# Two pieces of TensorE's work moved inside one step of an attention stage

## The reference

```
x = x + xattn0(ctx, layernorm(x))     # 16 heads of 16: softmax(q k^T / 4) v, then w_out and b_out
x = x + ffn0(layernorm(x))            # gate logits = xn @ gate_w.T + gate_b; the top 2 of 8 are counted,
                                      # and relu(xn @ W_e + b_e) is averaged over experts by those counts
x = x + xattn1(layernorm(x), ctx)     # one head of 256, with the mask
x = x + ffn1(layernorm(x))            # 8 experts, top 2, softmax weights
```

## Time and profile before

| | us |
|---|---|
| median of 3 runs | 973.59 (972.66 to 981.06) |
| the profiled execution | 976.29 |
| its span, first to last instruction | 974.4 |
| first stage, steps with all work (300 to 350 us of the span): PE busy | 50.00 of 50.00 |
| the same: DVE, ACT, POOL busy | 43.22, 37.10, 28.86 of 50.00 |

### The profile page before, as it was taken

The page is one execution under the profiler, slowest core; times in us unless marked ns, Lnnn a source line. Parts: engine busy times, 40 slices in busy tenths (PEclk is TensorE's granted clock), DMA queues, the critical chain, the costliest instruction groups (busy, mean ns, idle before and its releaser), DMA issues. The chain is left out here.

```text
span 974.4 us, 31409 instructions
## 1 busy us (share of the span) xinstructions
PE 896.9 (92%) x10664; PEld 666.5 (68%) x10664; DVE 728.6 (75%) x2063; ACT 550.2 (56%) x1112; POOL 540.1 (55%) x865
## 2 busy tenths in 40 slices
PE   4799999999999999986999999999986399999993
PEld 2477777777777777755466666666654288989893
DVE  6578888888888888875768888888876356666673
ACT  4377777777777777664234444444456155555551
POOL 6655556555555565501036777777775535656536
PEclk9799999999999999997999999999998599999997
DMA  5544445444445445322475556566753447886535
GB/s 152 167 143 144 136 141 143 149 132 132 142 143 145 131 141 148 100 63 68 142 192 163 181 185 187 185 188 201 221 166 120 123 122 177 182 194 97 96 64 61
DMA packets 107278, 140.56 MB, mean 144 GB/s; under 512 B 23929, under 2 KB 92592, under 8 KB 106928
## 3 DMA queue, kind: packets, MB, share of 16 engines
q1 hardware_dynamic: 94594, 121.38, 42.1%
q0 software_dynamic: 12528, 17.18, 9.7%
HBM read 93.38 MB, written 38.35 MB: 135 GB/s over the span
## 5 line engine op out<-in xcount | busy, mean ns | idle before, releaser
L997 DVE TENSOR_REDUCE smax<-psum 112x2 f32<-112x750 f32 x240 | 216.2, 933 | 24.8 <-PE psum L439 24.7
L838 ACT ACTIVATE probsT<-psum 125x896 f32<-125x896 f32 x173 | 158.7, 917 | 21.6 <-PE psum L454 20.2
L2660 POOL DMA_INDIRECT out_dram<-y,token_at x63 | 101.1, 1604 | 94.2 <-DMA out_dram<-y,token_at 41.7
L2136 DVE SCALAR_TENSOR_TENSOR acc<-psum,neg_bias,acc 128x448 f32<-128x448 f32 x112 | 75.9, 679 | 10.8 <-PE psum L1695 10.6
L439 PE MATMUL psum<-k_stack,q_stack 63*128 63x375 f16 x480 | 69.8, 328 | 3.4 <-DVE smax L997 2.8
L1695 PE MATMUL psum<-xT_hi,we_hi 128*128 128x448 f16 x256 | 70.2, 356 | 1.1 <-ACT we_hi L1911 1.1
L476 PE MATMUL psum<-probsT,v_aug 125*32 125x112 f32 x2688 | 70.2, 260 | 0.1
L1695 PE MATMUL psum<-xT_lo,we_hi 128*128 128x448 f16 x256 | 69.9, 355 | 0.0
L1695 PE MATMUL psum<-xT_hi,we_lo 128*128 128x448 f16 x256 | 69.8, 354 | 0.0
L476 PEld LDWEIGHTS psum<-probsT,v_aug 125*32 125x32 f32 x2688 | 63.5, 110 | 8.9 <-ACT v_aug L864 8.5
L454 PE MATMUL psum<-q_stack,k_stack 64*128 64x112 f16 x1384 | 63.7, 211 | 1.8 <-DMA q_stack<-neg_max 1.8
(11 more groups left out here) (380 smaller groups left out, 2477.7 us busy)
## 6 DMA issues: line engine op xcount, KB each, us to landing
we<-in_ctxT_dram SPq DMA_DIRECT2D x34, 375.0 KB, 3.5
k_stack<-k_hi_dram SPq DMA_DIRECT2D x64, 188.0 KB, 2.9
ctx_rows<-in_ctx_dram SPq DMA_DIRECT2D x31, 375.0 KB
ctxT<-in_ctxT_dram SPq DMA_DIRECT2D x30, 375.0 KB
w_raw<-in_w_dram SPq DMA_DIRECT2D x32, 256.0 KB, 3.9
rows_e<-dispatch_dram SPq DMA_DIRECT2D x24, 272.0 KB, 3.1
k_hi_dram<-k_hi SPq DMA_DIRECT2D x32, 188.0 KB, 2.8
k_lo_dram<-k_lo SPq DMA_DIRECT2D x32, 188.0 KB, 3.1
```

The costliest lines, as they stand in the source:

```text
L838: nc.scalar.activation(probsT[:, p, c, hg, :, :, :].rearrange("p k h q -> p k (h q)"), psum[0:KC, 0:2, 0:4 * S], ACT.Exp, scale=float(HD) ...
L997: nc.vector.reduce_max(smax[:, (u - LAG_B) % 2, 2 * (s % 4) + s // 4::PAIRS], psum[0:S, pair_bank(s):pair_bank(s) + 2, 0:KV], AX.X).then_i ...
L2136: nc.vector.scalar_tensor_tensor(out, psum[:, mix_bank(t, u, k), 0:GT], neg_bias[:, hc, e:e + 1], out, ALU.max, ALU.add).then_inc(m["acc_r ...
L2660: nc.gpsimd.indirect_dma_start(dram["out"], bass.IndirectOffsetOnAxis(token_at[:, unit // PAIR % TOKEN_TURNS, unit % PAIR:unit % PAIR + 1] ...
```

## The change

In a step of the first stage, TensorE's `gate` moves from behind `pair_scores(7)` to behind `keys(1)`, ahead of `pair_scores(6)`, `unit_scoresT(3)` and `pair_scores(7)`; and `turn_maxima` moves from behind `vals(1)` to ahead of it. Nothing is added or removed. The lists of the other engines are the same, row for row.

```diff
                 keys(1)
+                if e:
+                    gate()
                 pair_scores(6)
                 unit_scoresT(3)
                 pair_scores(7)
-                if e:
-                    gate()
                 if d:
                     out()
                 if more:
                     new_norm(t, u + 1)
                 vals(0)
                 unit_scoresT(4)
-                vals(1)
                 if b_:
                     turn_maxima()
+                vals(1)
                 vals(2)
```

## The result

| | us, median | before beside it | ratio to before, 95% interval |
|---|---|---|---|
| the change, first comparison | 970.15 (13 runs) | 976.34 (13 runs) | 0.9938 [0.9922, 0.9955] |
| the same kernel, with the second set of experiments | 972.98 (12 runs) | 975.95 (29 runs) | 0.9975 [0.9952, 0.9998] |
| the same kernel, a third time | 971.6 (10 runs) | 976.81 (20 runs) | 0.9950 [0.9931, 0.9969] |

The change made the kernel faster, by 2.4 to 6.1 us in three comparisons, 4.5 on their mean. That is inside the forecast range (970.15 against 969.0 to 975.2) and within 1%. The size was forecast too small: -2.2 us. That 971.4 came within 1.3 us is luck: it was counted from 973.59, the median of the first three runs of before. The 13 runs of before have 976.34, and -2.2 from there is 974.1, still in the range but 4 us above what was measured.

A forecast was written before the change was run, and what follows sets the result against it. PE was taken to bound the first stage, busy throughout the full steps; -2.9 us over 26 full steps, +0.4 in step 3 and +0.3 in step 31 gave -2.2 from the median 973.59: 971.4 us, range 969.0 to 975.2.

The forecast's parts named there:

- What bounds the stage: First stage, full steps: PE sets the pace; its only wait is 0.06 us, `pair_scores(7)` behind maximum 5.
- The gate's price: Full steps: moving the gate behind `keys(1)` gains 0.08 us a step, between 0 and 0.1.
- the drain's row: Drain, same pair of blocks: scores start 0.115 us behind the gate's last product; taken for `pair_scores(6)` behind the gate.
- The transpose: Full steps: turned maxima ahead of `vals(1)` gain 0.03 us a step, between 0 and 0.05.
- The sum over the loop: 26 full steps, each 0.11 us shorter by rows: -2.9 us.
- The ends: Pipeline not full: +0.4 us in step 3, 0 in step 2, +0.3 (0 to 0.3) in step 31.
- the drain of short products eats the gain: Rival at the gate: scores wait until its last product ends; -0.5 to +0.7 us, 973 to 974.3; chance 0.30.
- DVE becomes the pace: Rival: the transpose waits for maximum 7 in full steps; 975 to 976, or 978; chance 0.10.
- less margin than I thought: Full step: maximum 7 was to end 0.4 us before the transpose is reached, so no wait.
- more comes back: Rival: full 0.1 and 0.05 us a step, -3.9, or the slow stretch shortened; 968 to 970; chance 0.13.

The follow-up runs named there:

- the gate alone: Against before, only the gate moved behind `keys(1)`, with the transpose of the maxima left in its old place: 0.9962 [0.9945, 0.9980].
- late-low-half kernel: Against before, only DVE's order changed, with maximum 5 taken ahead of `onT_lo`: 0.9986 [0.9967, 1.0004].

## Why the prediction was right, and where its size was off

- **What bounds the stage: right.** The only wait of PE that I had found, 0.06 ahead of `pair_scores(7)`, is gone after the change, and taking it away by itself is worth 0.07 to 0.08 a step.
- **The gate's price: the term that was mis-sized.** I took 0.08 us a step, between 0 and 0.1; it is 0.12 (12.97 to 12.85 with the gate alone), outside those bounds. The scores behind the gate came as the drain's row had it: 0.18 behind the start of the gate's last pair, 0.17 in the earlier trace rows. What I had too high was the front of the gate. I carried its 0.33 us over from the place behind the changed array. Behind `keys(1)` its first two pairs take 0.18 (302.33 to 302.51) instead of the 0.22 at 0.055 a product. The weight loads show the difference, first before, then in the changed kernel:

```profile
307.90 0.18 PEld L496 LDWEIGHTS psum<-gate_whi,xT_hi 128*112 128x112 f16 x2 [0.17 <-issue]
```

```profile
302.17 0.29 PEld L496 LDWEIGHTS psum<-gate_whi,xT_hi 128*112 128x112 f16 x2
```

Behind the changed array the gate's first load starts with its first product, at 307.90; behind `keys(1)` it starts 0.16 ahead of it, while the keys' last products run. With the price of the change of array behind it, the gate costs 0.36 there (302.33 to 302.69); in its old place its 0.33 came on top of the 0.09 behind `keys(1)`. The scores behind it stand 0.16 and 0.20 apart, where I took 0.17 and 0.21, which is another 0.02. `out` as the first behind the scores pays 0.02, as allowed for.
- **The transpose: right, at the end of its bounds.** 0.05 of 0 to 0.05, where I took 0.03. With the transpose and its 16 columns of weights at the head of the stretch, `vals(1)` takes what `vals(2)` takes without the change of array behind it: 0.66, against 0.65.
- **The sum over the loop.** 26 steps gave -4.1 to -4.2 us in three traces; I had -2.9. The two terms above make the difference.
- **The ends: right.** +0.25 to +0.45 in step 3 (0.4 forecast), +0.2 to +0.27 at the drain's start (DVE's first norm there 9.75 us behind step 31's transposed norm before, 10.02 after; 0.3 forecast). For step 2, where nothing was forecast, no loss can be told from what the start takes from run to run: from its transpose to the first transposed scores of step 3 it is 4.67 us before, and 4.79, 4.70 and 6.80 in the three traces of the change.
- **The rivals.** That the drain of short products eats the gain fell: the scores start at 302.69, ahead of the recorded end of the gate's last pair (302.75). The Trainium skill's "TensorEngine Tiling (Array Packing)", Tiling Modes, Key Properties, has the array drain at a change of tiling mode; the trace shows a price at each change, but less of it behind short products, not more: 0.07 (0.18 for the gate's last pair, less 0.11 at 0.055 a product) against 0.09 behind the keys. That DVE becomes the pace fell for these runs, with less margin than I thought. That more comes back, 0.15 a step, is what happened, with 0.17.

By place the change is worth -4.1 + 0.35 + 0.25 = -3.5 us. The timed -2.4 and -4.9 have it in their intervals, the first -6.1 [-7.6, -4.4] has not. The profiled spans differ by 8.3 (974.4 and 966.1), of which 1.7 lie ahead of step 5 and 2.3 behind step 31. Neither belongs to the change by what the other traces show: from step 31's transposed norm to the end the twelve traces took from 563.6 to 573.1 us, and the changed kernel alone 566.2, 570.7 and 572.5. I therefore hold the first comparison for one that came out high by chance. That is not shown; shown is only that nothing in the traces carries more than the 3.5.

## What to carry to other kernels

Where one engine is busy throughout, look at the distances between starts, and compare each with the same pair of blocks elsewhere in the list: a wait of 0.06 us that no idle time shows was worth 1.75 us in 26 steps. In this kernel a short piece of work on that engine was cheapest where it delays an instruction that waits anyway, and right ahead of a change in how the array is used; put among like products it gained nothing. Before moving it, work out the margin of what it waits for, since past the margin the wait is paid in each step (0.32 late, 0.34 longer), and treat the first and last steps, where the pipeline is not full, apart.

## What the runs showed of the hardware

- The first block of whole-array products behind products on half the rows takes longer: 0.70 against 0.66 for `vals` with 125 columns of weights, 0.70 against 0.68 for `out`; a transpose with 16 columns in front took it off. The first weight load there starts with its product (307.90 and 310.15 before), and not ahead of it as in the middle of a stretch; that this load is the whole of the price is likely, but no run shows it apart.
- Eight-column products took between 0.27 and 0.33 us for six, by neighbours: 0.33 behind the changed array, 0.29 among whole-array products, and 0.27 (0.36 less the 0.09 of the change) between whole-array products and a change.
- `xn` on DVE (L1015) took 0.40 us in before and 0.68 in the step shown of the changed kernel, with the same operands; the mean over the loop is 0.43 and 0.53, and 0.43 with the gate alone. In the changed kernel it starts maximum 6 some 0.25 us later than the scores would let it, which no wait of PE shows. What `xn` takes goes with POOL's `k_lo`, though `xn` waits for no semaphore of it; that an engine holds up the other there is the plain reading, and by what means no run shows. Before, then the changed kernel, to be laid beside `xn` at 302.71 above:

```profile
306.85 0.90 POOL L408 TENSOR_TENSOR k_lo<-we,k_hi 128x375 f16<-128x375 f32 x1
...
307.49 0.40 DVE L1015 TENSOR_SCALAR xn<-x_res,ln_mv,ln_rstd 112x256 f32<-112x256 f32 x1
```

```profile
302.35 0.90 POOL L408 TENSOR_TENSOR k_lo<-we,k_hi 128x375 f16<-128x375 f32 x1
```

`xn` ends 0.14 behind the end of POOL's `k_lo` in both (307.89 and 307.75, 303.39 and 303.25). In the loops of nine of the traces it ends 0.13 to 0.16 behind it wherever it takes more than 0.43, up to 0.91 us where it starts 0.14 into `k_lo`. So the earlier it starts within `k_lo`, the longer it takes, and in the late-low-half kernel, where DVE reaches it earlier, it takes 0.72 on the mean. Why POOL stands 0.28 later in the step shown of the changed kernel (from `keys(1)` to `k_lo` 1.00, 0.72 before) isn't followed up.
